# Router and gate weights of a two-layer transformer kernel: high and low part side by side as one stationary operand of 16 columns, the two halves of the logits added on VectorE

## The reference

```python
# layer 0, expert part: router over 8 experts
logits = einsum('bsh,eh->bse', x, router_w) + router_b
weights = softmax(logits); top-2 ...
# layer 1, expert part: gate over 8 experts
scores = sigmoid(xf @ gate.T)
... group choice, top-2, normalised scores, eight small experts, a shared expert
```

## Time and profile before

| | |
|---|---|
| median of 3 runs | 1983.21 us (1981.7 to 1983.69) |
| profiled execution, its own time | 1987.34 us |
| its span, first to last instruction | 1985.5 us |
| mean granted TensorE clock | 0.974 of full speed |
| busy: PE, DVE, ACT, POOL | 1850.5, 1359.2, 872.3, 846.6 us |

### The profile page before, as it was taken

How to read it: one execution, slowest core, us unless ns; L and a number is a source line. 1 busy time by engine, 2 the same in 40 slices (tenths; PEclk the granted TensorE clock), 3 DMA queues, 4 the chain that set the end, 5 groups by cost and what they waited for, 6 DMA issues and landing times.

```text
span 1985.5 us, 35384 instructions
## 1 busy us (share of the span) xinstructions
PE 1850.5 (93%) x11696; PEld 1619.0 (82%) x11728; DVE 1359.2 (68%) x3178; ACT 872.3 (44%) x1623; POOL 846.6 (43%) x1144
## 2 busy tenths in 40 slices
PE   7999998399999986999999999999999999999996
PEld 6888887288888975878878878878878878878885
DVE  5688887644444436876886786786786786786664
ACT  4445554323333334355445445445445445444443
POOL 4267777531111013265265255255255256255054
PEclk9999999599999987999999999999999999999998
DMA  3111221322233232121112112112112113111011
GB/s 133 65 64 64 85 86 44 107 72 88 89 96 100 81 111 62 33 71 59 43 60 70 43 51 80 40 47 86 38 49 87 38 49 86 36 52 54 11 43 65
DMA packets 81004, 130.98 MB, mean 66 GB/s; under 512 B 11200, under 2 KB 62016, under 8 KB 80736
## 3 DMA queue, kind: packets, MB, share of 16 engines
q1 hardware_dynamic: 71984, 104.96, 15.7%
q0 software_dynamic: 8880, 24.26, 5.1%
HBM read 104.52 MB, written 24.67 MB: 65 GB/s over the span
## 4 chain that ended last, share of the span: by engine, by line
PE 44%; DVE 6%; issue 5%; POOL 4%; ACT 3%; POOLq 0%; DVEq 0%; DMA 0%; ACTq 0%
PE c_ps L118 10%; PE c_ps L120 9%; PE c_ps L119 9%; PE c_ps L127 3%; PE c_ps L128 3%; PE c_ps L129 3%; PE c_ps L1924 2%; PE c_ps L1985 2%; PE c_ps L1987 1%; PE c_ps L1986 1%; POOL c_pool_tmp L97 1%; ACT c_x L1526 1%; DVE c_place L1755 1%; DVE c_tmp L97 1%; DVE c_shared_place L1842 1%
## 5 line engine op out<-in xcount | busy, mean ns | idle before, releaser
L1465 POOL TENSOR_TENSOR c_place<-c_shared_place,c_place 128x512 fp32r<-128x512 f32 x256 | 326.0, 1301 | 195.0 <-ACT c_place L1642 109.9
L1456 POOL DMA_INDIRECT c_gathered<-expert_results,c_slots x112 | 112.4, 1004 | 326.7 <-DVE c_pre L1691 303.2
L1842 DVE SCALAR_TENSOR_TENSOR c_shared_place<-c_ps,c_shared_place 128x512 f32<-128x512 f32 x256 | 170.4, 683 | 48.8 <-ACT c_shared_place L1634 48.6
L118 PE MATMUL c_ps<-c_place 128*128 128x256 f32 (+1 forms) x520 | 149.2, 287 | 16.6 <-DVE c_place L1860 9.8
L127 PE MATMUL c_ps<-c_downT_hi,c_place 128*128 128x256 f32 x512 | 149.8, 293 | 8.9 <-POOL c_place L1465 8.9
L1642 ACT ACTIVATE c_place<-c_shared_place 128x512 fp32r<-128x512 f32 x128 | 80.3, 630 | 171.6 <-DVE c_shared_place L1842 170.6
L120 PE MATMUL c_ps<-c_place 128*128 128x256 f32 (+1 forms) x520 | 147.9, 284 | 0.0
L119 PE MATMUL c_ps<-c_place 128*128 128x256 f32 (+1 forms) x520 | 147.8, 284 | 0.0
L1021 POOL DMA_INDIRECT b_xs<-x_rows,expert_tokens x56 | 57.8, 1032 | 204.8 <-PE b_ps L1153 143.6
L128 PE MATMUL c_ps<-c_downT_lo,c_place 128*128 128x256 f32 x512 | 142.6, 278 | 0.0
L129 PE MATMUL c_ps<-c_downT_hi,c_place 128*128 128x256 f32 x512 | 142.4, 278 | 0.0
(11 more groups left out here) (404 smaller groups left out, 6106.6 us busy)
## 6 DMA issues: line engine op xcount, KB each, us to landing
c_x2T<-score_rows SPq DMA_DIRECT2D x64, 512.0 KB, 5.3
a_xT_raw<-xT SPq DMA_DIRECT2D x8, 1024.0 KB, 6.4
a_x_rows<-x SPq DMA_DIRECT2D x8, 1024.0 KB, 5.6
x_rows<-a_x SPq DMA_DIRECT2D x8, 1024.0 KB, 4.4
c_pre<-x_rows SPq DMA_DIRECT2D x8, 1024.0 KB
out<-c_x SPq DMA_DIRECT2D x16, 512.0 KB, 3.0
b_win_raw<-w_in SPq DMA_DIRECT2D x7, 1024.0 KB, 5.8
b_wout_raw<-w_out SPq DMA_DIRECT2D x7, 1024.0 KB
```

Of the source, the lines that this page charges most:

```text
L118: pe.matmul(out, lh, rh, start=(j == 0), stop=False)
L1456: pool.indirect_dma_start(rows[:, a, :], None, d["ys"], bass.IndirectOffsetOnAxis(ap=slots[:, a, t:t + 1], axis=0), bounds_check=TRASH + P ...
L1465: pool.tensor_tensor(hid_lo[:, place, :], square[:, place % RING, :], f32(hid_hi[:, place, :]), ALU.subtract).then_inc(hid_split, 1)
L1842: v.scalar_tensor_tensor(square[:, place % RING, :], ps[:, s_bank(unit, k - lag), :], 0.0, factor, ALU.max, ALU.mult).then_inc(s_free, 1)
```

## The change

The low part of the router's and of the gate's weights is put into the same tensor as the high part, 8 + 8 columns (`wr`, and `gateT` with 16 columns). A logit unit is now four matmuls, each with the 16-column stationary operand, once on the high and once on the low part of the rows; its output is 16 x 512. (This also adds the product lo·lo, which was left out before.) The transposes give 16 columns for each tile. The two halves of 8 are added by a `tensor_reduce` on VectorE, a new instruction in both routes. In stage a the reduce frees the bank, and the scaling that read PSUM now reads its result. In stage c the reduce stands ahead of ScalarE's exp, which waits for it and reads its result `summed` from SBUF. The parts around it have new step counts. The core of the diff:

```diff
-        wr_hi, wr_lo = pair("wr", [P, CH, EXPERTS])
+        wr = sb("wr", [P, CH, 2, EXPERTS], F32R)
...
-                v.tensor_tensor(logit[:], bank[:, 0:TILES * EXPERTS].rearrange("p (t e) -> p t e", e=EXPERTS), across(scale[:], EXPERTS), ALU.mult).then_inc(bank_free, 1)
                 chain = Chain(v, route_chain, i * ROUTE_STEPS)
+                both = bank[:, 0:2 * TILES * EXPERTS].rearrange("p (t w e) -> p t e w", w=2, e=EXPERTS)
+                v.tensor_reduce(logit[:], both, AX.X, ALU.add).then_inc(bank_free, 1)
                 v.wait_ge(bank_free, n + 1)
-                chain.step(v.tensor_tensor(logit[:], logit[:], logit_shift[:], ALU.add))
+                chain.step(v.tensor_tensor(logit[:], logit[:], across(scale[:], EXPERTS), ALU.mult))
+                chain.then(v.tensor_tensor, logit[:], logit[:], logit_shift[:], ALU.add)
...
-                        product(pe, opened(unit)[0:EXPERTS, :], [(wr_hi[:, c, :], wr_lo[:, c, :], x1T_hi[:, c, bass.ts(j, HALF)], x1T_lo[:, c, bass.ts(j, HALF)])
-                                                                 for c in range(CH)]).then_inc(bank_full, 1)
+                        out = opened(unit)[0:2 * EXPERTS, :]
+                        for n, (c, rows_of) in enumerate((c, rows_of) for c in range(CH) for rows_of in (x1T_hi, x1T_lo)):
+                            last = pe.matmul(out, wr[:, c].rearrange("p w e -> p (w e)"), rows_of[:, c, bass.ts(j, HALF)], start=(n == 0), stop=(n == 2 * CH - 1))
+                        last.then_inc(bank_full, 1)
...
-                            last = pe.transpose(out[:, bass.ts(t, EXPERTS)], logit_e[:, bass.ts(t, P)], ident[0:EXPERTS, 0:EXPERTS])
+                            last = pe.transpose(out[:, bass.ts(t, 2 * EXPERTS)], logit_e[:, bass.ts(t, P)], ident[0:2 * EXPERTS, 0:2 * EXPERTS])
...
                     elif kind == "gateT":
-                        act.wait_ge(v_full, v_number(b, V_AT[unit]) + 1)
-                        wait_past(act, score_done, 2 * b + j)
-                        act.activation(expd[:].rearrange("p t e -> p (t e)"), ps[:, v_bank(unit), 0:HTILES * EXPERTS], ACT.Exp, scale=-1.0).then_inc(exp_done, 1)
+                        act.wait_ge(v_free, v_upto(b, unit))
+                        act.activation(expd[:], summed[:], ACT.Exp, scale=-1.0).then_inc(exp_done, 1)
...
+                v.wait_ge(v_full, n + 1)
+                v.tensor_reduce(summed[:], ps[:, v_bank(("gateT", h)), 0:2 * HTILES * EXPERTS].rearrange("p (t w e) -> p t e w", w=2, e=EXPERTS), AX.X, ALU.add).then_inc(v_free, 1)
                 v.wait_ge(exp_done, 2 * b + h + 1)
-                v.tensor_scalar(expd[:], expd[:], 1.0, None, ALU.add).then_inc(v_free, 1)
-                v.wait_ge(v_free, n + 1)
-                chain.step(v.reciprocal(score[:], expd[:]))
+                chain.step(v.tensor_scalar(expd[:], expd[:], 1.0, None, ALU.add))
+                chain.then(v.reciprocal, score[:], expd[:])
...
-                        product(pe, v_open(pe, b, unit)[0:EXPERTS, :], [(gate_hi[:, c, :], gate_lo[:, c, :], x3T_hi[:, c, :], x3T_lo[:, c, :]) for c in range(CH)]).then_inc(v_full, 1)
+                        out = v_open(pe, b, unit)[0:2 * EXPERTS, :]
+                        for n, (c, rows_of) in enumerate((c, rows_of) for c in range(CH) for rows_of in (x3T_hi, x3T_lo)):
+                            last = pe.matmul(out, gate[:, c, :], rows_of[:, c, :], start=(n == 0), stop=(n == 2 * CH - 1))
+                        last.then_inc(v_full, 1)
```

More of the change, by code:

```diff
@@ L575, in body @@
                         act.wait_ge(bank_full, number(i, unit) + 1)
-                        act.activation(logit_e[:, bass.ts(j, HALF)], ps[0:EXPERTS, bank_of(i, unit), :], ACT.Copy).then_inc(logit_copied, 1)
+                        act.activation(logit_e[:, bass.ts(j, HALF)], ps[0:2 * EXPERTS, bank_of(i, unit), :], ACT.Copy).then_inc(logit_copied, 1)
                     elif kind == "logitT":
@@ L596, in _ @@
             act.wait_ge(weights_in, 16 * 5)
-            for hi, raw in ((wq_hi, wq_raw), (wp_hi, wp_raw), (wr_hi, wr_raw)):
-                act.activation(hi[:], raw[:], ACT.Copy).then_inc(weights_hi, 1)
+            for hi, raw in ((wq_hi[:], wq_raw), (wp_hi[:], wp_raw), (wr[:, :, 0, :], wr_raw)):
+                act.activation(hi, raw[:], ACT.Copy).then_inc(weights_hi, 1)
             act.wait_ge(consts, CONSTS)
@@ L611, in _ @@
         def _(v):
[L612 removed]
+            for j, (lo, raw, hi) in enumerate(((wkv_lo[:], wkv_raw, wkv_hi[:]), (wq_lo[:], wq_raw, wq_hi[:]), (wp_lo[:], wp_raw, wp_hi[:]), (wr[:, :, 1, :], wr_raw, wr[:, :, 0, :]))):
                 v.wait_ge(weights_hi, j + 1)
[L614 removed]
+                v.tensor_tensor(lo, raw[:], f32(hi), ALU.subtract).then_inc(weights_split, 1)
             v.wait_ge(consts, CONSTS)
@@ L1266, in stage_c @@
         wqk_hi, wqk_lo = pair("wqk", [P, CH, C])
-        (gate_hi, gate_lo), (fc1_hi, fc1_lo), (fc2_hi, fc2_lo) = weights["gateT"], weights["fc1T"], weights["fc2T"]
+        gate, (fc1_hi, fc1_lo), (fc2_hi, fc2_lo) = weights["gateT"][0], weights["fc1T"], weights["fc2T"]
         (w1_hi, w1_lo), (up_hi, up_lo), (down_hi, down_lo) = weights["w1T"], weights["upT"], weights["downT"]
@@ L1295, in stage_c @@
         comb_hi, comb_lo = pair("comb", [P, HALF])
-        logit = sb("logit", [EXPERTS, HALF])
+        logit = sb("logit", [2 * EXPERTS, HALF])
+        summed = sb("summed", [P, HTILES, EXPERTS])
         gathered = sb("gathered", [P, GATHER, 2, C])
@@ L1802, in body @@
                         v.wait_ge(v_full, n + 1)
-                        v.tensor_copy(logit[:], ps[0:EXPERTS, v_bank(unit), :]).then_inc(v_free, 1)
+                        v.tensor_copy(logit[:], ps[0:2 * EXPERTS, v_bank(unit), :]).then_inc(v_free, 1)
                     elif kind == "gateT":
@@ L1947, in body @@
                         for t in range(HTILES):
-                            last = pe.transpose(out[:, bass.ts(t, EXPERTS)], logit[:, bass.ts(t, P)], ident[0:EXPERTS, 0:EXPERTS])
+                            last = pe.transpose(out[:, bass.ts(t, 2 * EXPERTS)], logit[:, bass.ts(t, P)], ident[0:2 * EXPERTS, 0:2 * EXPERTS])
                         last.then_inc(v_full, 1)
@@ L2025, in program @@
         stage_a(nc, d, inv)
-        shapes = {"wv": [P, CH, C + 2], "gateT": [P, CH, EXPERTS], "fc1T": [P, CH, LATENT], "fc2T": [P, 1, C],
+        shapes = {"wv": [P, CH, C + 2], "gateT": [P, CH, 2 * EXPERTS], "fc1T": [P, CH, LATENT], "fc2T": [P, 1, C],
                   "w1T": [P, EXPERTS, P], "w2T": [P, EXPERTS, LATENT], "upT": [P, CH, SHARED], "downT": [P, SHARED // P, C]}
-        weights = {name: tuple(ctx.enter_context(nc.sbuf_tensor(f"c_{name}_{part}", shape, F32R)) for part in ("hi", "lo")) for name, shape in shapes.items()}
+        weights = {name: tuple(ctx.enter_context(nc.sbuf_tensor(f"c_{name}_{part}", shape, F32R)) for part in ("hi", "lo")[:1 if name == "gateT" else 2]) for name, shape in shapes.items()}
         first_slots, first_gates = (ctx.enter_context(nc.sbuf_tensor(f"c_{name}", [P, n, TILES], dt)) for name, n, dt in (("slots", 2, U32), ("gates", 3, F32)))
-        stage_b(nc, d, [(d[name], hi[:, :, 0:C], lo[:, :, 0:C]) if name == "wv" else (d[name], hi, lo) for name, (hi, lo) in weights.items()],
+        gate = weights["gateT"][0]
+        halves = {**weights, "gateT": (gate[:, :, 0:EXPERTS], gate[:, :, EXPERTS:2 * EXPERTS])}
+        stage_b(nc, d, [(d[name], hi[:, :, 0:C], lo[:, :, 0:C]) if name == "wv" else (d[name], hi, lo) for name, (hi, lo) in halves.items()],
                 first_slots, first_gates, inv)
```

6 lines of the change are left out of this document (3 added, 3 removed).

## The result

| | |
|---|---|
| this, median of 20 runs | 1985.14 us (1983.43 to 1986.32) |
| before, median of 20 runs beside them | 1982.41 us (1980.52 to 1983.83) |
| ratio | 1.0014, 95% interval 1.0008 to 1.0020 |
| profiled execution of this, and its span | 1986.08 us, 1984.3 us |

The change costs 2.7 us; the forecast was a gain of 4.9 us, and 1985.14 lies outside its range. One warning before the traces are compared: the profiled execution of before was 4.9 us above the median of these runs of before, that of this only 0.9 above its own. Stage b explains it. So stage a and stage c are compared by themselves.

The account below looks back on a forecast made before the run. PE bounds stage a's full steps, VectorE that stage's end, and a relay between engines stage c. Stage a -5.56 + 0.15 + 0.5 = -4.9 us and stage c 0.0 gave 1978.3 us, range 1974.5 to 1982.0.

Parts of the forecast that it names:

- Stage a: Six full steps save 5.56 us of matmuls, transposes cost 0.15, the reduce 0.5 at the end: -4.9 us.
- Matmuls of 0.232 us, not 0.131: Stage a's logit matmuls priced at 0.232 us from the rows; rival at 0.131 gives -2.5 us, 1980.7, chance 0.03.
- LAST and TAIL: End of stage a: eight saved matmuls buy nothing as PE waits for VectorE; two reduces add 0.5 us.
- Stage c's own two gates: Stage c's two gate units: eight times +0.06 us at the first, less 0.46 once at the second, 0.0 us.
- gate 0: First gate unit of a stage c batch: relay gains 0.45 us, reduce, exp and handovers cost 0.51, net +0.06.
- gate 1's 0.46 us: Second gate unit in stage c: PE's saving goes into its bank wait in seven batches, counts only in the last.
- Stage c: ... 0.0 us: Sum for stage c: 8 times +0.06 us, less 0.46 in the last batch, is 0.0 us.
- steady batches keep their 150.5 us: Sign of being right: stage c's steady batches stay at 150.5 us.
- a batch longer by over 0.2 us: Sign of being wrong: a batch of stage c longer or shorter by over 0.2 us.
- The relay costs more: Rival, stage c's first gate: 0.3 to 0.9 us a batch over seven batches, 1980.4 to 1984.6 us; chance 0.22.
- slower: Rival, stage c's first gate: reduce and addition take 1.05 us each under POOL's work, +8.8, 1992.0 us; chance 0.05.

Follow-up runs that it names:

- three pairs at one place: Kernels with and without stage a's part or the whole change, idle instructions aligning VectorE's loop code; medians 4.8, 4.3 and 4.6 us apart, the last two 5.0 by ratios.
- after_pad8: The changed kernel with 8 idle instructions on VectorE ahead of stage c's loop; 1985.80 us, ratio 0.9985 to the kernel before (1988.70 beside it).
- turns_p8: The whole change, loop head at 1100, with VectorE also waiting for POOL's scale ahead of combine 6; 1992.40 us, ratio 1.0052 to the kernel before.
- the first table: Four runs: changed kernel plus 8 idle instructions, before plus 7, stage a's part alone, stage c's part alone; ratios 0.9985, 1.0043, 0.9998, 1.0016 to before.

## Why the prediction was wrong

**Stage a, right.** Matmuls of 0.232 us, not 0.131, a reduce of 0.30 for 0.25; LAST and TAIL gave nothing. Forecast -4.9 us, measured -4.3, -4.8 and -5.0 in three pairs at one place.

**Stage c's own two gates, right.** Net nothing at gate 0 (addition of 1 at 8.24 us behind PE's restart for 8.19), gate 1's 0.46 us lost in the wait of 0.79. Forecast 0.0, measured -0.4 with the interval around nothing. A small thing was not seen: PE's transposes now wait 0.33 us for `c_logit`, which is part of the same 0.46.

**The step that failed** is the term "Stage c: ... 0.0 us", with its "steady batches keep their 150.5 us": everything in the loop but the two gates was put at nothing, without a reason. Batches behind a jump took 152.1 us. The prediction's own sign of being wrong, a batch longer by over 0.2 us, came. Two things moved with VectorE's instruction count. The stop at instruction 1095 came to lie between the splits of q: 5.7 us, by `after_pad8`. And the kernel before stood at a good place: its copy with 18 idle instructions takes 1.0012 of its time, 2.4 us more. POOL's scale takes 5.15 us in the loop of the kernel before and 5.66 in that copy; why the place decides this is not shown. -4.6 + 5.7 + 2.4 is 3.5 us (3.1 with the ratios' -5.0), measured 2.7, within the intervals (0.06 to 0.1% each, 1 to 2 us). None of the rivals held it. "The relay costs more" would have reached to 1984.6 and "slower" was on the right side, but at gate 0 no new small instruction took more than 0.23 us, so neither mechanism was there. The trace of before did show the first stop, 1.73 us of idle DVE put down to issue where its loop begins; it was read past, since PE did not wait for it. That the net came out as small as 2.7 us is chance: it is what three terms of 2 to 6 us leave of each other.

## What to carry to other kernels

Read idle time put down to "issue" at a loop's head, and ask what stands some instructions further; instructions added anywhere ahead on that engine shift other work onto a second stop. A change of less than 0.5% in a kernel with a loop of over 500 instructions on one engine, as here, should be timed at two or three places of the code, with idle instructions ahead of the loop on both sides, before a gain or loss is believed. Here the change, worth 4.6 us, measured as 2.7 us of loss. And before one engine is made to wait for another, ask whether TensorE's stop behind it gets long: at 3.7 us the granted clock fell with it here.

## What was not expected of the hardware

- VectorE behind a jump back: 1.7 to 2.0 us until its first instruction, then a stop of 0.22 to 1.18 us between instructions 1094 and 1096 of its program, with the head at 1089 and at 1091. Another of 0.35 us stands in front of instruction 1351 with the head at 1100, with and without a jump back ahead.
- VectorE's sum of two SBUF operands (128x256, 0.48 us) takes 1.03 to 1.56 us beside POOL's subtractions of 128x512, and the other way round POOL's 15 instructions of 128x4 take 4.43 us alone and 5.15 or 5.67 beside VectorE's sums.
- Behind TensorE's stops of 3.7 us in `turns_p8` the granted clock was 0.50 for 3.4 or 6.8 us, in each of seven batches.
- PE's stops in stage b did not go with the kernel: five in one trace of before (0.45 to 0.92 us), none in another. All four traces of the first table have five to seven of them, 3.3 to 3.7 us in all, a stage b of 359 to 360 us instead of 353 to 355, and the kernel before took 1988.70 us beside them; no trace of a later table has any, and there it took some 1982 us. Those tables came from other chips; whether the chip is the cause no run shows.
